# Transposing the normalised conv output in two halves of 64 rows, each in its own half of TensorE and its own PSUM bank

## What is computed

```
x = x + conv3x3_int8(groupnorm16(x), weight) + bias
x = x + irfft2( R * rfft2(groupnorm16(x))[32 x 16 lowest modes] )
```

## Time and profile before

| what | value |
|---|---|
| median of 3 runs | 3604.74 us (3603.62 to 3613.89) |
| the profiled execution's own time | 3599.9 us |
| its span in the profile | 3598.1 us |
| PE, DVE, ACT busy | 85%, 86%, 66% of the span |

### The profile page before, as it was taken

How to read it: one execution, slowest core, us unless ns; L and a number is a source line. 1 busy time by engine, 2 the same in 40 slices (tenths; PEclk the granted TensorE clock), 3 DMA queues, 4 the chain that set the end, 5 groups by cost and what they waited for, 6 DMA issues and landing times.

```text
span 3598.1 us, 81875 instructions
## 1 busy us (share of the span) xinstructions
PE 3060.9 (85%) x33273; PEld 1524.8 (42%) x33273; DVE 3091.9 (86%) x3288; ACT 2371.9 (66%) x3523; POOL 695.4 (19%) x1040
## 2 busy tenths in 40 slices
PE   5666666599999999999999999688888888888886
PEld 1111111266666666666666666433222222222222
DVE  6999999998898989898898989399888888888887
ACT  6888888689898888889898988433333333333332
POOL 0000000144344444444443444000000000000000
PEclk7777777799999999999999999799999999999998
DMA  9999999899999999999999999499999999999998
GB/s 398 421 422 421 421 421 421 271 362 362 308 351 341 347 331 344 344 346 356 317 366 312 356 335 327 159 384 427 427 427 427 427 427 427 427 427 427 427 423 370
DMA packets 342542, 1352.57 MB, mean 376 GB/s; under 512 B 45792, under 2 KB 47040, under 8 KB 243808
## 3 DMA queue, kind: packets, MB, share of 16 engines
q1 hardware_dynamic: 223104, 811.13, 60.0%
q0 software_dynamic: 82272, 268.58, 20.4%
q10 hardware_dynamic: 36864, 268.45, 17.7%
HBM read 811.10 MB, written 536.87 MB: 375 GB/s over the span
## 4 chain that ended last, share of the span: by engine, by line
PE 44%; DMA 41%; DVE 6%; ACT 4%; issue 3%; SPq 1%; DVEq 0%; ACTq 0%
DMA out<-ring 20%; PE ps L732 18%; PE ps L743 13%; DMA ring<-x_scratch 9%; DMA ring<-in_x 8%; PE ps L753 7%; DMA x<-in_x 3%; ACT area L320 3%; DVE ring L669 3%; PE ps L694 2%; DMA mixb<-in_x 1%; DVE stat L485 1%; PE ps L770 1%; PE ps L777 1%; DMA vbuf<-in_x 1%
## 5 line engine op out<-in xcount | busy, mean ns | idle before, releaser
L296 POOL DMA_DIRECT2D x_scratch<-ring x1024 | 689.4, 680 | 1565.1 <-DVE ring L580 1543.3
L884 PE MATMUL ps<-x,gj_s 128*128 128x512 bf16 x3072 | 772.8, 405 | 210.7 <-DVE ring L669 209.7
L580 DVE SCALAR_TENSOR_TENSOR ring<-ps,sc,ring 128x1024 f32<-128x1024 f32 x512 | 650.5, 1282 | 158.1 <-PE ps L732 151.3
L669 DVE TENSOR_TENSOR ring<-ps,ring 128x1024 f32<-128x1024 f32 x512 | 603.0, 1219 | 157.5 <-DMA ring<-x_scratch 154.6
L732 PE MATMUL ps<-area,wq 128*32 128x512 bf16 x12264 | 716.8, 381 | 13.7 <-DVE area L575 8.7
L345 ACT ACTIVATE area<-ps 128x512 f32<-128x512 f32 x1024 | 556.2, 599 | 182.5 <-PE ps L743 176.3
L884 PEld LDWEIGHTS ps<-x,gj_s 128*128 128x128 bf16 x3072 | 294.4, 102 | 766.8 <-DVE ring L669 438.5
L485 DVE TENSOR_REDUCE stat<-area 128x1 f32<-128x4096 f32 x128 | 565.3, 4416 | 45.1 <-ACT area L320 44.2
L743 PE MATMUL ps<-id_s,ring 128*128 128x128 f32 x4096 | 559.6, 280 | 6.5 <-ACT area L345 4.2
L352 ACT ACTIVATE area<-ring,qtab 128x2048 bf16<-128x2048 f32 x256 | 517.0, 2019 | 0.0
L743 PEld LDWEIGHTS ps<-id_s,ring 128*128 128x128 f32 x4096 | 441.5, 141 | 162.1 <-issue 153.6
(11 more groups left out here) (137 smaller groups left out, 2187.3 us busy)
## 6 DMA issues: line engine op xcount, KB each, us to landing
ring<-in_x SPq DMA_DIRECT2D x1024, 256.0 KB, 7.4
x_scratch<-ring POOLq DMA_DIRECT2D x1024, 256.0 KB, 6.7
ring<-x_scratch SPq DMA_DIRECT2D x256, 1024.0 KB, 11.0
out<-ring ACTq DMA_DIRECT2D x256, 1024.0 KB, 25.8
ring<-in_x SPq DMA_DIRECT2D x148, 1024.0 KB, 20.3
vbuf<-in_x SPq DMA_DIRECT2D x36, 1024.0 KB, 21.0
mixb<-in_x SPq DMA_DIRECT2D x36, 1024.0 KB, 21.1
x<-in_x SPq DMA_DIRECT2D x36, 1024.0 KB, 21.1
```

The source lines that it names most:

```text
L296: pool.dma_start(x1_rows[b, m, r], xslot(t % XS)[32 * r:32 * r + 32, :].rearrange("p (g w) -> p g w", g=4)).then_inc(s_x_out[t % XS], 16)
L580: nc.vector.scalar_tensor_tensor(out=half, in0=ps[0][:, h * HF:(h + 1) * HF], scalar=col(26), in1=half, op0=ALU.mult, op1=ALU.add).then_in ...
L669: nc.vector.tensor_tensor(half, ps[0][:, hj * 2 * HW:(hj + 1) * 2 * HW], half, ALU.add).then_inc(s_add, 1)
L884: last = mm(bank(j), gj_s[:, (j * 3 + v) * 128:(j * 3 + v + 1) * 128], (z12, z12, z13)[v][:, k % 2], start=(v == 0), stop=(v == 2))
```

## The change

`turn_x1` makes each 128 x 128 transpose as two: rows 0 to 63 of the chunk with the upper left 64 x 64 of the identity, and rows 64 to 127 with the lower right. The weights are then 64 rows by 128 columns and the output is 128 x 64. All upper halves go to bank 4 and all lower halves to bank 5; the two banks together now hold the result of two v (a pair), so `s_t` and `s_te` count pairs, and every wait on them is rewritten. ACT still makes four copies of 512 elements for each chunk, but a copy takes one bank and scatters it in runs of 64 elements. On PE the halves of `conv` are moved: half 0 stands between the pairs, half 1 behind the second one, and the even `turn_rows` stands behind half 0.

```diff
             def turned(t, pair):
+                act.wait_ge(s_t, 2 * t + pair + 1)
+                if t >= 2 and pair == 0:
                     act.wait_ge(s_w, t - 1)
-                act.activation(xt[:, t % 2, v], bank(4 + v % 2), ACT.Copy).then_inc(s_te, 1)
+                for k in range(2):
+                    last = act.activation(
+                        xt[:, t % 2, 2 * pair:2 * pair + 2].rearrange("p v (g k m) -> p k (v g) m", g=4, k=2)[:, k],
+                        bank(4 + k).rearrange("p (s m) -> p s m", m=64), ACT.Copy)
+                last.then_inc(s_te, 1)
...
             def turn_x1(t, v):
                 if v == 0:
                     pe.wait_ge(s_ev, 2 * t + 2)
-                if 4 * t + v >= 2:
-                    pe.wait_ge(s_te, 4 * t + v - 1)
+                if t or v:
+                    pe.wait_ge(s_te, 2 * t + v // 2)
                 for g in range(4):
-                    last = nc.tensor.transpose(bank(4 + v % 2)[:, 128 * g:128 * g + 128],
-                                               xslot(t % XS)[:, g * HW + 128 * v:g * HW + 128 * v + 128], id_s[:])
-                last.then_inc(s_t, 1)
+                    for k in range(2):
+                        c0 = 256 * (v % 2) + 64 * g
+                        last = nc.tensor.transpose(bank(4 + k)[:, c0:c0 + 64],
+                                                   xslot(t % XS)[64 * k:64 * k + 64,
+                                                                 g * HW + 128 * v:g * HW + 128 * v + 128],
+                                                   id_s[64 * k:64 * k + 64, 64 * k:64 * k + 64])
+                if v % 2:
+                    last.then_inc(s_t, 1)
...
                 if 4 <= i and i - 4 < T:
                     turn_x1(i - 4, 0)
                     turn_x1(i - 4, 1)
+                if 2 <= i and i - 2 < T:
+                    conv(i - 2, 0)
                 if small and j < 4:
                     turn_rows(b, 2 * j)
-                if 2 <= i and i - 2 < T:
-                    conv(i - 2, 0)
-                    conv(i - 2, 1)
                 if 4 <= i and i - 4 < T:
                     turn_x1(i - 4, 2)
                     turn_x1(i - 4, 3)
+                if 2 <= i and i - 2 < T:
+                    conv(i - 2, 1)
```

More of the change, by code:

```diff
@@ L250, in _ @@
                 sp.wait_ge(s_x_out[(t - 1) % XS], ((t - 1) // XS + 1) * 64)
-                sp.wait_ge(s_t, 4 * t)
+                sp.wait_ge(s_t, 2 * t)
                 sp.wait_ge(s_ss, t)
@@ L257, in _ @@
             last = max(t for t in range(T) if 4 <= t % XS < 8)
-            sp.wait_ge(s_t, 4 * (last + 1))
+            sp.wait_ge(s_t, 2 * (last + 1))
             sp.wait_ge(s_ss, last + 1)
@@ L262, in _ @@
                 sp.wait_ge(s_x_out[k], len(range(k, T, XS)) * 64)
-            sp.wait_ge(s_t, 4 * T)
+            sp.wait_ge(s_t, 2 * T)
             sp.wait_ge(s_ss, T)
@@ L339, in scaled, with turned @@
                                scale=qtab[:, B + b:B + b + 1]).then_inc(s_ua, 1)
-            def turned(t, v):
-                act.wait_ge(s_t, 4 * t + v + 1)
-                if t >= 2 and v == 0:
+            def turned(t, pair):
+                act.wait_ge(s_t, 2 * t + pair + 1)
+                if t >= 2 and pair == 0:
                     act.wait_ge(s_w, t - 1)
-                act.activation(xt[:, t % 2, v], bank(4 + v % 2), ACT.Copy).then_inc(s_te, 1)
+                for k in range(2):
[3 more added lines that the diff above has]
+                last.then_inc(s_te, 1)
             def squared(t):
@@ L391, in _ @@
                     turned(i - 4, 0)
-                    turned(i - 4, 1)
                     squared(i - 4)
@@ L396, in _ @@
                 if 4 <= i and i - 4 < T:
-                    turned(i - 4, 2)
-                    turned(i - 4, 3)
+                    turned(i - 4, 1)
                 if small and j == 12:
@@ L739, in turn_x1 @@
                     pe.wait_ge(s_ev, 2 * t + 2)
-                if 4 * t + v >= 2:
-                    pe.wait_ge(s_te, 4 * t + v - 1)
+                if t or v:
+                    pe.wait_ge(s_te, 2 * t + v // 2)
                 for g in range(4):
-                    last = nc.tensor.transpose(bank(4 + v % 2)[:, 128 * g:128 * g + 128],
-                                               xslot(t % XS)[:, g * HW + 128 * v:g * HW + 128 * v + 128], id_s[:])
-                last.then_inc(s_t, 1)
+                    for k in range(2):
[6 more added lines that the diff above has]
+                    last.then_inc(s_t, 1)
             def along_w1(t):
-                pe.wait_ge(s_te, 4 * t + 4)
+                pe.wait_ge(s_te, 2 * t + 2)
                 if t >= 4 and t % 4 == 0:
@@ L765, in turn_rows @@
                 elif n == 1:
-                    pe.wait_ge(s_te, 4 * T)
+                    pe.wait_ge(s_te, 2 * T)
                 else:
```

## The result

The changed kernel takes 3622.39 us in the median of 20 runs (3605.19 to 3645.75), the kernel before 3605.45 us in 20 runs on the same chip (3600.51 to 3614.39). The ratio is 1.0041, with a 95% interval of 1.0031 to 1.0050. The forecast was 3540, the range 3505 to 3600: it missed, and on the wrong side.

What follows compares the result with a forecast made beforehand. PE was taken to set the pace of the middle stage. Gains of 36, 16 and 13 us, together 65, took 3599.9 to 3535; the median's 4.8 us more gave 3540, range 3505 to 3600.

Steps and rivals of the forecast that it cites:

- The transposes: Middle stage, PE: half transposes overlap in the array, 0.06 us a pair, so a block takes 0.63 us instead of 1.02.
- no overlap: Rival, chance 0.12: the array halves do not work side by side, a block takes 1.11 us instead of 1.02, total 3657.
- long weight load: Rival, chance 0.07: loading the weights is the long side, pairs run at 0.11 us as before, total 3600 to 3610.
- PE's step: Middle stage: PE's work in a plain step falls from 5.77 to 4.99 us.
- ACT and the hand-over: Copies keep their price, 1.08 us a pair; the moved convolution halves cover the roughly 1.4 us hand-over of both banks.
- DVE as the next limit: Plain steps: DVE's unchanged 5.42 us of work, say 5.45 with hand-overs, becomes the next limit.
- a step loses 0.78: 5.77 -> 4.99: PE in the middle stage: two shorter transpose blocks take 0.78 us off a step, with no added change of shape.
- 0.4 us to spare: PE's slack against DVE, 5.42 - 4.99 us a step, should the cover of the first pair's copies fail.
- Plain steps: Middle stage: mean falls from 5.77 to 5.58 us, between DVE's 5.45 and transfers' 5.72; 36 us over 192 steps.
- The steps after an image: Steps that finish an image: 32 with `turn_rows` go from 6.80 to 6.3 us, gaining 16; 32 others gain 13 us.
- The transfers' rival: Rival, chance 0.17: transfers hold the middle stage, plain steps stay at 5.7 us or more, total 3560 to 3590.

Runs made afterwards that it cites:

- the last experiment: Changed kernel with only the first transpose pair in halves, the second whole, turned x1 and width weights in bf16: 3544.4 us, ratio 0.9827 to the kernel before.

## Why the prediction was wrong

- **The transposes: right.** The halves overlap. 0.63 us was forecast for a block, 0.65 is measured; "no overlap" and "long weight load" fell with it. The 16 loads of a block take 0.58 us, less the 0.14 of one some 0.03 from load to load, 0.06 for a pair as forecast:

```profile
851.51 0.58 PEld L747 LDWEIGHTS ps<-id_s,ring 64*128 64x128 f32 x16 [0.20 <-issue]
```

- **PE's step: right where nothing interrupts it.** 4.99 was forecast, and the cycle from 848.58 to 853.57 us in the timeline above is 4.99. In the mean PE is recorded as busy for 5.2 us a step (67.77 us in thirteen); a stop alone adds to that, as the 24 convolution matmuls that one divides there are 0.83 + 1.03 us instead of 1.48.
- **ACT and the hand-over: right.** A copy takes 608 ns for 599, and with the pair signals alone the kernel is unchanged.
- **DVE as the next limit: right as a limit, not reached.** It has 5.44 us of work a step (70.74 in thirteen), and undisturbed steps run at 5.37 to 5.4.
- **The step that failed: "a step loses 0.78: 5.77 -> 4.99" in every step, with PE left "0.4 us to spare".** It took for granted that PE's time is the sum of what its array does, so the 32 more instructions in each step were priced at nothing. The runs show a price: at the stops the next 256 instructions took 6.7 to 7.0 us in the median to come. Before, PE used them up in 7.6 us; after, it would in 5.9 us of its own work, and it stopped at 106 of 234 places, 137 us in all. The rows had it: in the earlier trace rows `mix` issues 128 matmuls and 128 loads, 256 instructions, and then stands idle for 2.06 us with "issue" as the cause. I read that row for its 1.35 us and passed over the idle time.
- **Plain steps: 5.58 forecast, 5.70 measured**, a gain of 0.08 where 0.19 was forecast; in the last experiment, without stops but with less work on PE, they take 5.52. So the mean of 5.58, half way to what transfers seemed to allow, was within reach, and more than half of the gain did not come while there were stops: 58 us of idle PE in 139 steps, part of it beside DVE's work.
- **The steps after an image: 16 us forecast for `turn_rows` and 13 for the others.** In seven images steps 2 to 7 gained 7 us, which the order alone gives too, and steps 12 to 17 lost 34, with 30 stops and 56 us where the kernel before has 7 stops and 14 us. The prediction had a gain there and nothing for stops; this loss turns the sign. Some 12 us of it come with the order, 22 with the halves. The clock at 1.2 GHz behind the long stops is a part of it that was not measured apart.
- **The transfers' rival** (3560 to 3590) is not what holds the kernel: with nearly all stops gone, and the width transform in bf16, it reached 3544 at the same traffic.
- What stays open: why the packet starts 3.5 to 4.3 us after the place where the last chunk began and not earlier, and how much of that is other traffic; fewer stores brought it down, but no run took the traffic away altogether. It is open too why stops remain where a chunk has 7.05 us or more (the changed kernel with DVE longer, and in bf16).

## What to carry to other kernels

Splitting matmuls to use the array better doubles their instructions. Before doing it, divide PE's busy time in the stretch by its PE instructions, loads counted: here the plain steps had next to no stops above 27 ns each and some at 26.2 and below. A few stops need not cost the gain: half of the split (26 ns) made the kernel 0.7% faster, the whole (22.9 ns) 0.4% slower. In a profile, look for idle time with "issue" as its cause in the middle of a group of matmuls, 128 matmuls with their loads apart.

## What the runs showed that I had not expected

- One packet of 16384 bytes for each 256 PE instructions, with 2.4 to 2.7 us from its start to PE going on at a stop (medians of all runs); it starts 2.5 us (before) to 4.3 us (changed, after a stop) behind the last place. In the changed kernel 0.66 of the stops were followed by one at the next place, and 0.29 of the places without.
- A pause of PE at a wait helps only in part: 82 stops with DVE as the pace and the halves (106 with the halves alone), 9 without the halves.
- Long stops come with a lower clock: 55 us at 1.2 GHz in the stage where the kernel before has 7. One such stretch, at 1570.2 us, stands at the end of a stop of 4.39 us in the burst of `spectra`.
